# First stage of a Mamba and feed-forward block: layer norm statistics of three batches taken before the loop, skip term on GpSimd

## The reference, cut to what matters

```python
xn = _layernorm(x, axis=-1)            # (x - mean) / sqrt(var + 1e-5)
x = x + mamba(xn) + ffn(xn)

# mamba, with DI = 1024 channels, N = 16 states, K = 4 taps
proj = einsum('blh,eh->bel', xn, Win); hs, gate = proj[:, :DI], proj[:, DI:]
hs = silu(depthwise_conv(hs, Wconv, 4 taps) + bconv)
ssm_p = einsum('bdl,pd->blp', hs, Wx)          # dt_in (128), Bm (16), Cm (16)
dt = softplus(dt_in @ Wdt.T + bdt)
h_t = exp(A dt_t) * h_(t-1) + dt_t * Bm_t * hs_t;  y_t = sum_n h_t[n] * Cm_t[n]
y = (y + hs * D) * silu(gate)                  # hs * D is the skip term
out = einsum('bdl,hd->blh', y, Wout)
# ffn: gated gelu, 512 -> 2 x 2048 -> 512, in fp8
```

## Time and profile before

| | us |
|---|---|
| median of 3 runs | 1261.31 |
| the profiled execution, its own time | 1263.65 |
| its span in the trace | 1261.9 |
| of this: ahead of the loop's steady work | about 26 |
| batches 0 to 3 of `block_a` | about 26 to 241 |
| `block_b` | about 241 to 1262 |
| busy over the span: PE, DVE, ACT, POOL | 965.4, 1056.4, 760.7, 977.0 |

### The profile page before, as it was taken

One profiled execution on the slowest core, in us unless ns is written; L12 is line 12 of the kernel. 1 busy time (PEld: TensorE's weight loads), 2 busy tenths in 40 slices (PEclk: granted clock), 3 DMA queues, 4 the chain that ended last, 5 costly groups with the idle time before them and its releaser, 6 DMA issues.

```text
span 1261.9 us, 16993 instructions
## 1 busy us (share of the span) xinstructions
PE 965.4 (77%) x4304; PEld 577.9 (46%) x4304; DVE 1056.4 (84%) x1205; ACT 760.7 (60%) x1097; POOL 977.0 (77%) x783
## 2 busy tenths in 40 slices
PE   4888888467668787877677878776778787767888
PEld 3655555143344454444344544433445444434554
DVE  7877966588888998888789988887889888888994
ACT  4878786565666465666555655665546566656451
POOL 4342433698888799888788998887879988889792
PEclk9999999788888898988788988897879898889899
DMA  8665768861111137211111372111112721111100
GB/s 281 213 236 197 262 239 318 307 240 46 51 34 55 34 99 281 77 61 64 45 55 34 117 262 80 63 59 45 55 34 99 281 75 61 67 42 34 34 1 34
DMA packets 51603, 147.38 MB, mean 117 GB/s; under 512 B 5680, under 2 KB 14000, under 8 KB 48432
## 3 DMA queue, kind: packets, MB, share of 16 engines
q1 hardware_dynamic: 51504, 146.26, 33.2%
HBM read 108.23 MB, written 38.01 MB: 116 GB/s over the span
## 4 chain that ended last, share of the span: by engine, by line
POOL 51%; issue 20%; PE 4%; DVE 3%; ACT 2%; POOLq 1%; DVEq 0%
POOL dbu L920 38%; POOL hp L928 13%; DVE hp L974 1%; PE yT L1095 1%; PE mm L1053 1%; DVE da L974 1%; PE mm L1017 1%; DVE prod L943 1%; PE da L1017 1%; ACT L867 1%; ACT L863 1%; PE mm L1074 0%; POOLq L919 0%; ACT gate_bf L867 0%; ACT L868 0%
## 5 line engine op out<-in xcount | busy, mean ns | idle before, releaser
L879 ACT ACTIVATE da<-unit,neg_a 128x512 f32<-128x512 f32 x512 | 340.9, 686 | 354.8 <-DVE prod L943 344.5
L920 POOL TENSOR_TENSOR dbu<-unit,b_head 128x512 f32<-128x512 f32 x384 | 490.0, 1303 | 10.6 <-issue 5.8
L974 DVE TENSOR_TENSOR_SCAN da<-da,dbu 128x512 f32<-128x512 f32 x320 | 381.3, 1217 | 3.3 <-POOL dbu L920 2.3
L1095 PE MATMUL yT<-ident,prod 128*128 128x128 f32 x1280 | 225.1, 305 | 97.9 <-DVE prod L943 97.4
L974 DVE TENSOR_TENSOR_SCAN hp<-da,dbu 128x512 f32<-128x512 f32 x192 | 232.5, 1211 | 77.0 <-PE yT L1095 62.3
L928 POOL TENSOR_TENSOR hp<-hp,c_head 128x512 f32<-128x512 f32 x160 | 204.1, 1275 | 109.9 <-DVE hp L974 109.9
L1095 PEld LDWEIGHTS yT<-ident,prod 128*128 128x128 f32 x1280 | 163.2, 155 | 240.4 <-DVE prod L943 210.3
L1053 PE MATMUL mm<-xn_b,wffn 128*128 128x512 fp8e4 x512 | 160.0, 452 | 26.1 <-DVE acc L961 10.1
L920 POOL TENSOR_TENSOR dbu<-unit,b_all 128x512 f32<-128x512 f32 x128 | 160.1, 1275 | 0.0
L943 DVE TENSOR_TENSOR prod<-da,c_head 128x512 f32<-128x512 f32 x224 | 148.9, 665 | 0.0
L1095 PE MATMUL yT<-ident,hp 128*128 128x128 f32 x768 | 126.8, 292 | 0.0
(11 more groups left out here) (106 smaller groups left out, 1328.5 us busy)
## 6 DMA issues: line engine op xcount, KB each, us to landing
unit<-unit_d SPq DMA_DIRECT2D x32, 768.0 KB, 4.4
unit_d<-dt_du SPq DMA_DIRECT2D x32, 512.0 KB, 2.7
wf<-in_wffn SPq DMA_DIRECT2D x12, 1024.0 KB, 6.0
c_head<-bc_d SPq DMA_DIRECT2D x24, 512.0 KB, 5.4
b_head<-bc_d SPq DMA_DIRECT2D x18, 512.0 KB, 5.2
unit_d<-hsd SPq DMA_DIRECT2D x32, 256.0 KB, 4.0
wffn<-w_d SPq DMA_DIRECT2D x64, 128.0 KB, 3.9
wgate<-in_win_gate SPq DMA_DIRECT2D x32, 256.0 KB, 4.1
```

What stands on the lines that cost most here:

```text
L879: nc.scalar.activation(da[n % SLOTS][:, :], unit[:, k % 2, 0, :], ACT.Exp, scale=neg_a[:, k, n:n + 1]).then_inc(da_ready, 1)
L920: nc.gpsimd.tensor_tensor(dbu[:, n % DBUS, :], unit[:, k % 2, 1, :], b_all[n // NS][:, n % NS, :], ALU.mult).then_inc(dbu_ready, 1)
L974: nc.vector.tensor_tensor_scan(state, da[n % SLOTS][:, :], dbu[:, n % DBUS, :], 0.0, ALU.mult, ALU.add).then_inc(scanned, 1)
L1095: ins = nc.tensor.matmul(yT[k % 2][:, t * P:(t + 1) * P], product[:, t * P:(t + 1) * P], ident[:, :], start=False, stop=last, is_transpose ...
```

## The change

1. `statistics` takes a range of rows. Batch 0 has its own call as before. The 12 rows of batches 1 to 3 are done in one call ahead of the loop, behind the last cast of `win_hi` and ahead of `convolve(0, 0)`. `deviation` of the 12 rows stands on ACT behind `newest_tap(0, 0)` and ahead of the Exp for `neg_a`. The five small instructions for 1/sqrt are a function `invert`, called for the 12 rows right ahead of the loop. In the loop `normalise` has only its 4 instructions, which pick their columns by the batch number.
2. `skip_term` is gone from ACT. POOL makes `hsd(k)` by a tensor_scalar behind `hs_lo(k)`, with the same wait for the store of hsd(k-2).

`products` is unchanged. The semaphore counts follow. The diff without the sizes of the small tiles:

```diff
@@ gpsimd, body, for k in range(KU)
                     nc.gpsimd.tensor_tensor(hs_lo[:, k % 2, :], hs[:, k, :], hs_hi[:, k % 2, :], ALU.subtract).then_inc(hs_lo_ready, 1)
+                    pool.wait_ge(hsd_stored[k % 2], b * (16 * KU // 2) + 16 * (k // 2) + 16)
+                    pool.sem_inc(waited, 1)
+                    nc.gpsimd.tensor_scalar(hsd[:, k % 2, :], hs[:, k, :], cols_sb[:, k, C_D:C_D + 1], None,
+                                            ALU.mult).then_inc(hsd_ready, 1)
@@ vector
-            def statistics(x_tile):
-                for t in range(LT):
+            def statistics(rows, x_tile):
+                for t in rows:
                     ins = nc.vector.bn_stats(out=stats[:, t, :], in_=x_tile(t))
 ...
-            def normalise(b, x_tile):
-                dve.wait_ge(sd_ready, b + 1)
-                link(nc.vector.reciprocal(rstd[:, :], sd[:, :]))
+            def invert(rows):
+                some = slice(rows[0], rows[-1] + 1)
+                link(nc.vector.reciprocal(rstd[:, some], sd[:, some]))
+                link(nc.vector.tensor_tensor(newton[:, some], rstd[:, some], rstd[:, some], ALU.mult))
+                link(nc.vector.tensor_tensor(newton[:, some], newton[:, some], vare[:, some], ALU.mult))
+                link(nc.vector.tensor_scalar(newton[:, some], newton[:, some], -0.5, 1.5, ALU.mult, ALU.add))
+                link(nc.vector.tensor_tensor(rstd[:, some], rstd[:, some], newton[:, some], ALU.mult))
+            def normalise(x_tile, column):
                 for t in range(LT):
-                    ins = nc.vector.tensor_scalar(xn[:, t, :], x_tile(t), moments[:, t, 0:1], rstd[:, t:t + 1],
+                    ins = nc.vector.tensor_scalar(xn[:, t, :], x_tile(t), column(moments, t), column(rstd, t),
                                                   ALU.subtract, ALU.mult)
@@ vector, ahead of the loop
                 nc.vector.tensor_copy(win_hi[:, k, :], win_sb[k % WINS]).then_inc(win_hi_ready, 1)
+            dve.wait_ge(x_rest_loaded, 16 * (B - 1))
+            statistics(range(LT, B * LT), lambda t: x_rest[:, t - LT, :])
             dve.wait_ge(const_loaded, 32)
 ...
-            dve.wait_ge(x_rest_loaded, 16 * (B - 1))
+            dve.wait_ge(sd_ready, 2)
+            invert(range(LT, B * LT))
@@ vector, body
-                    if k == 2 and not last:
-                        statistics(next_tile)
                     if k == 3 and not last:
                         dve.wait_ge(xn_used, b + 1)
-                        normalise(b + 1, next_tile)
+                        normalise(next_tile, next_column)
@@ scalar, ahead of the loop
             newest_tap(0, 0)
+            deviation(2, slice(LT, B * LT))
             act.wait_ge(alog_loaded, 16)
             nc.scalar.activation(neg_a[:, :, :], neg_a[:, :, :], ACT.Exp).then_inc(neg_a_ready, 1)
@@ scalar, body
-                def skip_term(k):
 ...
                     high_part(k - 1)
-                    if k >= 2:
-                        skip_term(k - 2)
-                    if k == 3 and not last:
-                        deviation(b + 1)
 ...
                 high_part(KU - 1)
-                skip_term(KU - 2)
 ...
-                skip_term(KU - 1)
```

More of the change, by code:

```diff
@@ L109, in block_a @@
         x_rest = c_head
[L110 to L112 removed]
+        stats = sb("stats", [P, B * LT, 6])
+        moments = sb("moments", [P, B * LT, 2])
+        vare, sd, rstd, newton = (sb(n, [P, B * LT]) for n in ("vare", "sd", "rstd", "newton"))
         xnT = sb("xnT", [P, HT, L])
@@ L309, in statistics @@
                 dve.sem_inc(waited, 1)
-                for t in range(LT):
+                for t in rows:
                     ins = nc.vector.bn_aggr(out=moments[:, t, :], in_=stats[:, t, :])
                 link(ins)
-                nc.vector.tensor_scalar(vare[:, :], moments[:, :, 1], EPS, None, ALU.add).then_inc(var_ready, 1)
-            def normalise(b, x_tile):
-                dve.wait_ge(sd_ready, b + 1)
-                link(nc.vector.reciprocal(rstd[:, :], sd[:, :]))
[L320 to L323, removed]
+                some = slice(rows[0], rows[-1] + 1)
+                nc.vector.tensor_scalar(vare[:, some], moments[:, some, 1], EPS, None, ALU.add).then_inc(var_ready, 1)
+            def invert(rows):
+                some = slice(rows[0], rows[-1] + 1)
+                link(nc.vector.reciprocal(rstd[:, some], sd[:, some]))
[4 more added lines that the diff above has]
+            def normalise(x_tile, column):
                 for t in range(LT):
-                    ins = nc.vector.tensor_scalar(xn[:, t, :], x_tile(t), moments[:, t, 0:1], rstd[:, t:t + 1],
+                    ins = nc.vector.tensor_scalar(xn[:, t, :], x_tile(t), column(moments, t), column(rstd, t),
                                                   ALU.subtract, ALU.mult)
@@ L336, in _ @@
             dve.wait_ge(x_loaded, 16)
-            statistics(lambda t: xn[:, t, :])
-            normalise(0, lambda t: xn[:, t, :])
+            statistics(range(LT), lambda t: xn[:, t, :])
+            dve.wait_ge(sd_ready, 1)
+            invert(range(LT))
+            normalise(lambda t: xn[:, t, :], lambda rows, t: moments[:, t, 0:1] if rows is moments else rstd[:, t:t + 1])
             for k in range(KU):
@@ L366, in next_tile, with next_column @@
                     return x_rest[:, bass.ds(b * LT + t, 1), :].rearrange("p o h -> p (o h)")
-                links[0] = b * (LN_LINKS + KU * CONV_LINKS) + LN_LINKS + CONV_LINKS
+                def next_column(rows, t):
+                    if rows is moments:
+                        return moments[:, bass.ds(b * LT + LT + t, 1), 0:1].rearrange("p o m -> p (o m)")
+                    return rstd[:, bass.ds(b * LT + LT + t, 1)]
+                links[0] = b * (KU * CONV_LINKS) + links_before
                 for k in range(KU):
@@ L427, in copy_tiles, with deviation @@
                     nc.scalar.activation(xnT[:, h, :], tp[h % 2][:, :], ACT.Copy).then_inc(xnT_ready, 1)
-            def deviation(b):
-                act.wait_ge(var_ready, b + 1)
-                nc.scalar.activation(sd[:, :], vare[:, :], ACT.Sqrt).then_inc(sd_ready, 1)
+            def deviation(which, some):
+                act.wait_ge(var_ready, which)
+                nc.scalar.activation(sd[:, some], vare[:, some], ACT.Sqrt).then_inc(sd_ready, 1)
             act.sem_inc(xnT_ready, 2)
```

9 lines of the change are left out of this document (3 added, 6 removed).

## The result

The change makes the kernel slower: 1274.11 us median of 4 runs (1269.5 to 1276.77) against 1261.7 us, ratio 1.0092 with a 95% interval of [1.0061, 1.0124]. That is 11.6 us by the ratio, 12.4 by the medians. Five further rounds gave 1.0101 [1.0079, 1.0122]. The forecast was +3.4 us, 1264.7 us, with a range to 1269.0. The direction was right and the size was not.

A forecast was written before the change was run, and what follows sets the result against it. PE, busy throughout its runs, was taken to bound batches 0 to 2 of the first stage; 9.4 - 3 x 1.8 - 2.4 + 1.8 = +3.4 us on 1261.3 gave 1264.7 us, range 1260.0 to 1269.0 us.

The forecast's parts named there:

- prelude: Ahead of the loop: the 12-row statistics call delays the start of PE's run, +9.4 us, with ends 8.5 and 12.
- last batch: Last batch: hs_lo(6) and hs_lo(7) queue on POOL behind hsd waiting for stores, so ssm_inputs(7) comes later, +1.8 us.
- What bounds the stage: First stage: PE is busy throughout runs of some 20.6 us, so work taken off DVE or ACT inside buys 0 us.
- DVE is the bound: Rival: DVE paces the runs, so batches 0 to 2 each shorten by 4.1 us; sum -3.6 us, 1257.7 us, chance 0.12.
- The price of hsd on POOL: Each hsd tensor_scalar on POOL was put at 0.9 us, with ends of 0.5 and 1.28 us.
- The end of PE's run: Batches 0 to 2: ssm_inputs(7) 1.45 us earlier and the dt_in copy earlier, gaining 1.8 us a batch, three times.
- the case of no collision: Rival: POOL and DVE don't meet at hsd(6), gaining 2.4 us a batch; sum +1.6 us, 1262.9 us, chance 0.27.
- Waits for stores in batches 0 to 2: The store of hsd(3) leaves earlier and lands before hsd(5) needs it: cost 0, with 1.3 us to spare.
- this rival: Rival: a late store of hsd(3) holds hsd(5) and hs_lo(6) on POOL; sum +7.6 us, 1268.9 us, chance 0.18.
- The stall in batch 0: Batch 0: dt tile 4's wait of 4.13 us for the store of tile 0 should go, worth 2.4 us.
- one of the signs that the prediction named for being wrong: The prediction is wrong if PE waits for POOL inside a run.
- The clock in the runs: Lower PE clock, considered only for the prelude: its upper end of 12 us if PE is still on it in its run.

The follow-up runs named there:

- e11: Changed kernel with hsd on POOL made by a tensor_copy instead of a tensor_scalar, leaving out D; ratio 1.0027 to the kernel before.
- e3: Changed kernel with the skip term hsd made on DVE instead of POOL; ratio 0.9997 to the kernel before.
- e4: Changed kernel with the statistics call ahead of the loop cut from 12 rows to 4; ratio 1.0075 to the kernel before.
- e9: Changed kernel with DVE's cast of k = 7 moved behind low_tiles(0 to 2); ratio 1.0106 to the kernel before.
- second profile: The changed kernel run again with no edit; ratio 1.0101 to the kernel before.
- e2: Changed kernel with statistics put back into the loop, so only the skip term on POOL remains; ratio 1.0079 to the kernel before.
- e10: Kernel before with hsd(5) to hsd(7) on DVE and SP's load of B rows behind the sixth dt tile store; ratio 0.9932 to before.
- e1: Changed kernel with the skip term put back on ACT, so only the statistics ahead of the loop remain; ratio 1.0048 to the kernel before.
- e6: Kernel before with hsd(5) to hsd(7) still on ACT but placed later in its order; ratio 1.0176 to the kernel before.
- e7: Statistics in the loop as before, skip term on POOL one unit behind: hsd(k-1) behind hs_lo(k); ratio 1.0036 to the kernel before.

## Why the prediction was wrong, step by step

Each term is the distance between the starts of PE's runs in two batches, after against before:

| term | predicted | measured |
|---|---|---|
| prelude | +9.4 | +9.9 (45.04 - 35.14) |
| batch 0 | -1.8 - 2.4 | -2.8 (52.39 - 55.19) |
| batch 1 | -1.8 | +0.7 (53.27 - 52.61) |
| batch 2 | -1.8 | +1.4 (52.76 - 51.38) |
| last batch | +1.8 | +1.6 (50.33 - 48.74) |
| sum | +3.4 | +10.7 |

The table lumps what happened at the end of PE's run with what came behind it. The first alone is the distance from the start of a run to the start of its ssm_inputs(7), in us. An asterisk marks a run that was partly at the lower clock, which adds about 1.5 us to it:

| batch | before | changed | e11, copy on POOL | e3, hsd on DVE |
|---|---|---|---|---|
| 0 | 25.08 | 25.09 | 23.74 | 24.70* |
| 1 | 25.10 | 25.94 | 25.28* | 23.14 |
| 2 | 25.08 | 26.54* | 23.74 | 23.12 |

So of the 7.3 us between +3.4 and +10.7, 5.4 are the gain at the ends of three runs that did not come, 0.8 a wait for a store in batch 1, and 1.5 the clock in batch 2; the rest are smaller terms of both signs.

- *What bounds the stage: right.* At the full clock PE's run is 20.6 us before and after, and the work taken off DVE (2.1 to 3.8 us) and ACT (4.7 to 6.1 us) did not shorten it. The rival "DVE is the bound" is out (its sum has 12.4 for 3 x 4.1 = 12.3, which changes nothing).
- *Prelude: right in mechanism and size.* e4 shows it one for one.
- *The price of hsd on POOL: the step that failed first.* I took 0.9 us, "because this row is the nearest: same engine, one input", with ends of 0.5 and 1.28. It is 1.56 us, outside both ends, since I took the operation with two inputs for an upper end of one with one input. With 0.61 us in its place (e11) ssm_inputs(7) comes 1.34 us earlier than before in batches 0 and 2; with 1.56 us it doesn't come earlier at all.
- *The end of PE's run: the gain of 1.8 us a batch did not come.* The part on ACT was right: hs_hi(7) of batch 0 starts 2.0 us earlier against the start of the run. POOL used all of it up. hsd(6) began when the cast had 1.1 us left, as I had put it. Then come 1.56 us instead of 0.9, and 0.4 us more, which I didn't have: DVE's low part of a tile stands behind the cast, and e9 shows that such a pair holds each other up. hs_lo(7) then took 1.57 instead of 1.28 us beside the next low part. Of the 1.45 us that I forecast for ssm_inputs(7), the price takes 0.66 us and the low parts about 0.7. Where nothing stands on POOL (e3), ssm_inputs(7) comes 1.96 us earlier, close to the 2.05 us that I gave for the case of no collision. The Trainium skill, "SBUF — State Buffer", section "Who interferes with whom", says that a DVE instruction in a two-port mode, such as a cast can be, and a GpSimd instruction exclude each other for the whole instruction; the rows agree (3.05 us beside the cast, 1.56 us in batch 0 of e9 without it).
- *Waits for stores in batches 0 to 2: wrong for batch 1 of this execution.* "Cost 0, with 1.3 us to spare" was used up: hsd(5) waits 0.87 us there, and PE 2.07 us for hs_lo(6), which costs 0.8 us at ssm_inputs(7). In the second profile PE has no such wait in batch 1. With the full DVE of e2 this rival acts in full.
- *The stall in batch 0: it went, 4.13 to 0.41 us, and was worth 2.8 us, but not beside a gain at the end of the run.* Where that gain comes (e11, 1.34 us) the dt tiles are made earlier too, tile 4 waits 3.50 us again, and batch 0 is 2.8 us shorter all the same. The sum counted both, -1.8 and -2.4. Only e10, which moves the B rows out of the way, has both (50.86 against 55.19 us).
- *The last batch: right in size (+1.6), by luck.* ssm_inputs(7) starts 28.13 us behind the start of the run instead of 25.62, +2.5 us where I had +1.8; the price explains the 0.7, since one hsd stands on this chain. (The "+2.8" that the prediction gives for 1.28 us counts it twice; it should be +2.2.) The other 0.9 us came back through the clock: before, the matmuls of ssm_inputs(7) came at a pace of 0.43 us, and from its start to the first project_dt it took 4.08 us (219.94 to 224.02 us); in the changed kernel the last four came at 0.23 us, and it took 3.16 us (231.59 to 234.75 us). The timeline of PE before:

```profile
220.53 0.63 PE L521 MATMUL dt_ps<-hs_hi,wx_lo 128*128 128x512 f32 x1
220.96 0.63 PE L522 MATMUL dt_ps<-hs_hi,wx_hi 128*128 128x512 f32 x1
...
224.02 1.12 PE L563 MATMUL z_ps<-dtin,wdt_sb 128*128 128x512 f32 x2 [1.16 <-ACT bc L492]
```

  The wait of 1.04 us for hs_lo(3) inside the run is one of the signs that the prediction named for being wrong. What followed doesn't show it: hsd(5) started 22.0 us behind the start of the run, where ACT had started it after 22.3 us before.
- *The clock in the runs: missed.* The prediction had the lower clock only as an end of the prelude's range. Batch 2 of the first profile and all three batches of the second ran partly at the lower clock of 1.2 GHz, as these rows of batch 2 with their pace of 0.43 us show:

```profile
150.70 0.79 PE L526 MATMUL dt_ps<-hs_lo,wx_hi 128*128 128x512 f32 x1 [2.16 <-POOL hs_lo L286]
151.29 0.63 PE L527 MATMUL dt_ps<-hs_hi,wx_lo 128*128 128x512 f32 x1
151.72 0.63 PE L528 MATMUL dt_ps<-hs_hi,wx_hi 128*128 128x512 f32 x1
```

The granted clock of this run's first 20.6 us is 0.92. It adds about 1.5 us a batch: PE is busy for 24.05 to 24.2 us up to ssm_inputs(7) instead of 22.6. Without it batch 2 would be as long as before. It isn't tied to POOL: e1, e3, e6 and e10 have it in one or two batches too, and e7 to e9 and the one profile of the kernel before have none of it in these runs. Why it falls stays open. The idle time ahead of the run of batch 2 is 2.16 us before and after.

## What to carry to other kernels

Find the engine that is busy without a gap in the stretch, and ask of each edit whether it touches a place where that engine waits; work moved off its neighbours inside the stretch doesn't shorten it and can only help at its end (e1, 1.3 us a batch), and the same work placed ahead of the loop, where nothing covers it, costs its full time. When an operation goes to an engine on which the trace doesn't show that form, a form with more inputs is no upper bound, and what counts is who is queued behind it. Ask for every instruction of the other engine beside it, not only for the longest, whether the two hold each other up. An in-order queue of DMA issues turns one late tile into a late chain (e6, e9).

## What was not expected of the hardware

- On POOL, for 128x512 float32: tensor_scalar 1.49 us with a constant and 1.56 us with a column, tensor_tensor 1.28 us with two tensors and 1.04 us with one tensor twice, copy 0.61 us. DVE does the tensor_scalar in 0.49 us.
- A cast on DVE, 1.22 us alone, that began 0.4 us before the end of hs_lo(6) took 1.51 us, and the tensor_scalar on POOL, 1.56 us alone, that was issued during the cast took 3.05 us, with a low part of a tile behind the cast.
- That low part on DVE, a tensor_tensor of 0.69 us, holds POOL too: with no cast near, it took 1.51 us and the tensor_scalar on POOL 2.00 us (e9, batch 1).
- The changed kernel had one of its first three runs partly at the lower clock in one execution and all three in another. The run of batch 1 stood behind 2.16 us of idle time at the higher clock and behind 2.15 us at the lower one.
